# A two-layer graph convolution on one core: edge steps written out, gathers far ahead of the scatters, table clears interleaved with loads

## What is computed

```python
x = _layernorm(x + layer0(x, ...), axis=-1)
x = _layernorm(x + layer1(x, ...), axis=-1)
# in a layer:
h_s = s @ lin1_ws ;  h_v = einsum('nci,cd->ndi', v, lin1_wv)
w = silu(edge_scalars @ fc_w1) @ fc_w2
es = h_s[edge_src] ; ev = h_v[edge_src]        # gather by source
m_s1 = w1 * es * e0 ; m_v1 = (w2 * es)[:, :, None] * e1[:, None, :]   # and so on
agg = segment_sum(mid, edge_dst, num_segments=n)                      # scatter by destination
out = self connection of x + agg @ lin2, gated (layer 0) or scaled by alpha (layer 1)
```

## Time and profile before

| what | value |
|---|---|
| median of 3 runs | 2085.45 us (2083.66 to 2088.11) |
| span of the profiled execution | 2039.2 us |
| median less span, work that the span does not hold | 46.25 us |
| edge stage of layer 0, up to the first table read | 0 to 757 us |
| node stage of layer 0 | 757 to 1079 us |
| edge stage of layer 1 | 1079 to 1786 us |
| node stage of layer 1 | 1786 to 2039 us |

### The profile page before, as it was taken

One profiled execution on the slowest core, in us unless ns is written; L12 is line 12 of the kernel. 1 busy time (PEld: TensorE's weight loads), 2 busy tenths in 40 slices (PEclk: granted clock), 3 DMA queues, 4 the chain that ended last, 5 costly groups with the idle time before them and its releaser, 6 DMA issues.

```text
span 2039.2 us, 47736 instructions
## 1 busy us (share of the span) xinstructions
PE 1409.6 (69%) x10326; PEld 1244.3 (61%) x10326; DVE 1438.3 (71%) x5755; ACT 1048.9 (51%) x3502; POOL 1476.8 (72%) x1923
## 2 busy tenths in 40 slices
PE   5078887888888748888875999999998999300000
PEld 4067776777777637767654888888888888200000
DVE  5067777777777719999993666666666666299998
ACT  3034444444444418999983545445455445147766
POOL 4067888878888747888873677777777777468887
PEclk8589999998999969999987999999999999755555
DMA  9966666666666749999964777777777777499997
GB/s 388 429 155 134 135 138 135 136 133 136 137 134 135 178 102 333 338 340 337 337 221 131 167 170 170 169 168 174 170 172 169 169 173 163 84 366 401 403 399 290
DMA packets 253833, 439.51 MB, mean 216 GB/s; under 512 B 33424, under 2 KB 131152, under 8 KB 250576
## 3 DMA queue, kind: packets, MB, share of 16 engines
q1 hardware_dynamic: 152304, 311.47, 45.0%
q0 software_dynamic: 75264, 67.79, 24.0%
q10 hardware_dynamic: 26208, 59.65, 7.5%
HBM read 235.50 MB, written 203.27 MB: 215 GB/s over the span
## 4 chain that ended last, share of the span: by engine, by line
issue 23%; PE 19%; POOL 16%; DVE 11%; ACT 11%; another core or an unknown queue 6%; DMA 5%; SPq 5%; ACTq 2%; DVEq 1%; POOLq 0%
POOL table L500 7%; ACT y L849 6%; POOL xg L483 5%; DVE stats L1083 3%; SPq L374 3%; DVE res L1044 3%; DMA table<-sums,row_all 3%; PE ps L660 2%; PE ps L681 2%; POOL half_rstd L534 2%; DMA dst_row<-in_dst_row 2%; PE ps L641 2%; PE ps L627 1%; PE ps L643 1%
## 5 line engine op out<-in xcount | busy, mean ns | idle before, releaser
L500 POOL DMA_INDIRECT table<-sums,row_all x392 | 628.7, 1604 | 299.6 <-issue 131.0
L784 ACT COPY msg<-ps 128x192 f32<-128x192 f32 (+1 forms) x196 | 57.6, 294 | 703.5 <-PE ps L660 514.1
L849 ACT ACTIVATE y<-res,norm 128x160 f32<-128x160 f32 x756 | 330.2, 508 | 126.7 <-POOL norm L536 66.8
L993 DVE SCALAR_TENSOR_TENSOR x1g<-ps,a_all,x1g 128x160 f32<-128x160 f32 x392 | 132.4, 379 | 207.9 <-remote 139.7
L483 POOL DMA_INDIRECT xg<-in_x_rows,src_all x196 | 203.2, 1037 | 59.6 <-issue 58.1
L483 POOL DMA_INDIRECT xg<-x_rows,src_all x196 | 196.6, 1003 | 64.3 <-issue 57.3
L641 PE MATMUL ps<-weights,midT 128*128 128x128 f32 (+1 forms) x784 | 159.3, 286 | 67.6 <-DVE msg L953 67.0
L1083 DVE BATCH_NORM_STATS2 stats<-res 128x6 f32<-128x160 f32 x784 | 196.1, 312 | 2.6
L948 DVE TENSOR_TENSOR pe<-ps,ea_all 128x192 f32<-128x192 f32 x196 | 69.6, 355 | 166.8 <-ACT msg L784 89.7
L534 POOL TENSOR_TENSOR half_rstd<-var,minus_half 128x8 f32<-128x8 f32 x98 | 165.6, 1690 | 14.2
L641 PEld LDWEIGHTS ps<-weights,midT 128*128 128x128 f32 x784 | 123.8, 199 | 71.9 <-issue 64.4
(11 more groups left out here) (114 smaller groups left out, 4402.2 us busy)
## 6 DMA issues: line engine op xcount, KB each, us to landing
tab<-table SPq DMA_DIRECT2D x98, 384.0 KB, 5.2
table<-zeros SPq DMA_DIRECT2D x24, 1536.0 KB
table<-zeros SPq DMA_DIRECT2D x98, 324.0 KB
tab<-table SPq DMA_DIRECT2D x98, 324.0 KB, 5.6
xzT<-in_xzT SPq DMA_DIRECT2D x98, 320.0 KB, 4.9
x1g<-x_rows SPq DMA_DIRECT2D x98, 320.0 KB
base_rows<-x1g SPq DMA_DIRECT2D x98, 320.0 KB
x1g<-base_rows SPq DMA_DIRECT2D x98, 320.0 KB, 5.0
```

Source lines behind the costliest of these rows:

```text
L500: pool.indirect_dma_start(out=table[l], out_offset=bass.IndirectOffsetOnAxis(ap=row_all[:, at:at + 1], axis=0), in_=sums[j % 4][:, t, 0:W] ...
L849: last = nc.scalar.activation(y[u][:, t, :], res[u][:, t, :], ACT.Identity, scale=rstd[u][:, t:t + 1], bias=shift[u][:, t:t + 1])
L993: last = stt(x1g[v][:, 2 * b + t, :], n1_ps[:, t, :], a, x1g[v][:, 2 * b + t, :], ALU.mult, ALU.add)
```

## The change

`run_pairs` takes the place of `run_stages` in both edge stages on SP, PE, ACT and DVE: all 98 pairs are written out and there is no loop. The buffers of gathered rows grow from 8 to 30: 15 lie in the memory of `res` and 7 in that of `x1g`, tiles that the edge stages don't use otherwise (layer 1 uses the first four of `x1g`). The buffers of sums grow from 4 to 16, in the memory of `tab`. GpSimd gathers pairs up to `lead(l, n)` ahead of scatter n. SP loads `attrT` four pairs ahead, and clears table 0 with two transfers for each pair, each of which waits until the fourth transfer before it has landed.

```diff
+def run_pairs(base, stages):
+    for k in range(base, base + NP + max(lag for lag, _ in stages)):
+        for lag, f in stages:
+            if base <= k - lag < base + NP:
+                f(k - lag, k - lag - base, (k - lag) % RING)
...
+RES_SLOTS, X1_SLOTS = 15, 7
+XG_RING = RING + RES_SLOTS + X1_SLOTS
+SUM_RING = 16
+CLEARS0 = 25
...
+def lead(l, n):
+    return min(NP, 38 + n * 60 // 90 if l == 0 else 16 + n * 9 // 10)
...
+def clears0_by(m):
+    return 4 if m < 4 else min(CLEARS0, 4 + 2 * (m - 3))
...
+def clears1_by(m):
+    return max(0, min(NG, (m - 13) * NG // 82))
...
-                        for k in range(25):
+                        for k in range(clears0_by(m - 1) if m > 3 else 0, clears0_by(m)):
+                            if k >= 4:
+                                sp.wait_ge(s_zero0[k % 4], 16 * (k // 4))
...
-                    wait_count(pool, s_xgT, j - RING + 1)
+                    wait_count(pool, s_xgT, j - XG_RING + 1)
                     if l == 0:
-                        wait_count(pool, s_ea, j - RING + 1)
+                        wait_count(pool, s_ea, j - XG_RING + 1)
+                    if j >= RING:
+                        pool.wait_ge(s_gather[j % RING], landed(j - RING, j % RING, RING, 32))
...
-                for k in range(l * NP, (l + 1) * NP + RING):
-                    if k < (l + 1) * NP:
-                        gather(k)
-                    if k - RING >= l * NP:
-                        scatter(k - RING)
+                for n in range(NP):
+                    for k in range(lead(l, n - 1) if n else 0, lead(l, n)):
+                        gather(l * NP + k)
+                    scatter(l * NP + n)
```

More of the change, by code:

```diff
@@ L161, in program, with slots @@
         src_all = sb("src_all", [P, NP * 2], I32)
-        xg = [sb(f"xg{u}", [P, 2, D + 1]) for u in range(RING)]
+        res_all = sb("res_all", [P, RING * T * D])
+        x1g_all = sb("x1g_all", [P, RING * T * D])
+        tab_all = sb("tab_all", [P, RING * T * 192])
+        def slots(ap, n):
+            w = 2 * (D + 1)
+            return [ap[:, k * w:(k + 1) * w].rearrange("p (t c) -> p t c", t=2) for k in range(n)]
+        xg = ([sb(f"xg{u}", [P, 2, D + 1])[:, :, :] for u in range(RING)] + slots(res_all[:, :], RES_SLOTS) +
+              slots(x1g_all[:, 4 * T * D:RING * T * D], X1_SLOTS))
         attrT = eight("attrT", [P, P])
@@ L174, in program @@
         same1 = four("same1", [P, PAIR])
-        sums = four("sums", [P, 2, 192])
+        sums = [tab_all[:, k * 384:(k + 1) * 384].rearrange("p (t c) -> p t c", t=2) for k in range(SUM_RING)]
         prod = two("prod", [P, 2, 3 * V])
@@ L243, in program @@
         s_step = sem("constants_step")
-        s_zero = [sem(f"table{l}_zeroed") for l in range(2)]
+        s_zero0 = [sem(f"table0_zeroed{k}") for k in range(4)]
+        s_zero1 = sem("table1_zeroed")
         s_src = sem("src_loaded")
@@ L350, in _, with load_attr, load_attrs @@
                 base = l * NP
-                def load_attr(j, m, u, early=False):
-                    if l == 0 and isinstance(m, int) and 4 <= m < RING and not early:
-                        return
+                def load_attr(j, m):
                     wait_count(sp, s_hid, j - 7)
                     R2 = 2 * LAYERS[l]["R"]
-                    sp.dma_start(attrT[u][0:R2, :], A[f"attrT{l}"][bass.ds(m, 1)].rearrange("a k e -> k (a e)")).then_inc(s_attr[u], 16)
+                    sp.dma_start(attrT[j % RING][0:R2, :], A[f"attrT{l}"][m:m + 1].rearrange("a k e -> k (a e)")).then_inc(
+                        s_attr[j % RING], 16)
+                def load_attrs(j, m, u):
+                    if m == 0:
+                        for k in range(4):
+                            load_attr(j + k, k)
+                    if m + 4 < NP:
+                        load_attr(j + 4, m + 4)
                 def load_dst_row(j, m, u):
@@ L483, in gather @@
                         pool.indirect_dma_start(
-                            out=xg[j % RING][:, t, 0:width], out_offset=None, in_=rows,
+                            out=xg[j % XG_RING][:, t, 0:width], out_offset=None, in_=rows,
                             in_offset=bass.IndirectOffsetOnAxis(ap=src_all[:, at:at + 1], axis=0)).then_inc(s_gather[j % RING], 16)
@@ L494, in scatter @@
                     if j == l * NP:
-                        pool.wait_ge(s_zero[l], 16 * (25 if l == 0 else NG + 1))
+                        if l == 0:
+                            for k in range(4):
+                                pool.wait_ge(s_zero0[k], 16 * len(range(k, CLEARS0, 4)))
+                        else:
+                            pool.wait_ge(s_zero1, 16 * (NG + 1))
                     W = LAYERS[l]["ROW"]
@@ L770, in copy_z @@
                     wait_count(act, s_xgT, j - 1)
[L771 removed]
+                    copy(xz[u][:, :, :], xg[j % XG_RING][:, :, M:D]).then_inc(s_xz, 1)
                 def copy_xT(j, m, u):
```

62 lines of the change are left out of this document (31 added, 31 removed).

## The result

The changed kernel takes 2167.98 us (median of 4 runs, 2161.89 to 2177.17); the kernel before took 2085.87 us beside it. The ratio is 1.0397, with a 95% interval of 1.0365 to 1.0429: 4% slower, where no change was forecast, and outside the range.

A forecast was written before the change was run, and what follows sets the result against it. Two chains were taken to hold a pair: POOL's issue, some 6.45 us, and scatter after scatter, some 6.2. The terms +17 - 13.6 + 1 - 5 = -0.6 us gave 2084.9 us, own range 2074 to 2097, wider range 2062 to 2104.

The forecast's parts named there:

- from first to last scatter of layer 0: Layer 0's 97 steps: 60 with gathers at 6.57 us, 37 without at 6.25; -13.6 us, bounds -16 to -2.
- The sentence on the tail: Layer 0, behind the last gather: steps without gathers priced at 6.25 us, as clears of table 1 ran there too.
- First scatter: Start of layer 0: gathers and loads slow the clears, first scatter at about 125.7 us; +17 us, bounds +5 to +27.
- Layer 1: Layer 1's 97 steps: 642 us instead of 647.1, -5 us, bounds -12 to +2.
- eight between at 6.4: Layer 1: eight steps between the 82 with gathers and the last seven without, priced at 6.4 us each, 51.2 us.
- The fill: Layer 1, first gather to first scatter: four attrT loads now stand ahead of the first x1 load; +1 us.
- 46.25 us "around the span": Whole kernel: difference of the 2039.2 us span and the 2085.45 median, taken as unchanged.
- (a): Rival, edge stages: fetching the written-out code becomes the bound; slower, about 2122 us; chance 10%.
- (b): Rival, start: clears and gathers add up, +27, 2095 us; 2104 with steps without gathers at 6.5; chance 15%.
- (c): Rival: steps with gathers fall to 6.43 us, 2059; or clears lose nothing to gathers, 2073; chance 15% for both.
- (d): Rival, layer 0: the gathers' issue counts in full, saving 77 us, near 2010 us; chance 4%.
- (e): Rival: the lead does nothing, clears end as before and steps stay as they are; 2085 us; chance 5%.

The follow-up runs named there:

- unroll_no_pace: unroll_only without SyncE's wait, in layer 0, for scatter m-8 to land before it issues table 1's clear; 2173.63 us, ratio 1.0467.
- lead9_paced: clears_run_lead9 with one wait per pair for a scatter, ahead of layer 0's clears and in layer 1 ahead of the loads; 2041.48 us, ratio 0.982.
- unroll_only: The kernel before with the edge steps of both layers written out and nothing else; 2069.63 us, ratio 0.9996.
- clears_run_lead9: clears_run with gathers 9 pairs ahead in both layers, keeping 30 buffers of rows and 16 of sums; 2159.01 us, ratio 1.0422.
- clears_run: The changed kernel with table 0's clears in one run at pair 3, as before the change; 2177.37 us, ratio 1.0509.
- before_again: The kernel before, unchanged, timed and profiled anew; 2071.54 us, ratio 0.9994, its profiled execution 2072.37 us.

## Why the prediction was wrong

**The step that failed is the second, "from first to last scatter of layer 0", -13.6 us.** It took 53.2 us more instead. The prediction took the landing of a scatter to be as late as before, 6.20 to 6.57 us in every step. In the changed kernel 34 of the 77 steps counted had a clear beside the scatter and took 7.98 us, 1.49 more than the others; that is 51 of the 53 us. What was missed is that the diff dropped the wait in `clear_table1`. The prediction counted on table 1's clears to be harmless, since "clears of table 1 ran in it too"; those clears had been kept clear of the scatters by the wait. unroll_no_pace takes out that wait alone and layer 0's steps go from 638.2 to 734.4 us; lead9_paced puts it back and they go from 725.4 to 644.0.

The sentence on the tail was also a misreading. Its rows are those from 729 us on the earlier trace rows, and the last nine clears of table 1 had all been issued by then, in one run from 701.48 to 708.87:

```profile
701.48 7.39 SPq L381 DMA_DIRECT2D table<-zeros  x9
```

Nor is the idle of 5.19 us at 710.74 due to the end of the loop: with the loops written out the step at that place was still 8.27 us (unroll_only; 8.65 before). That those nine clears cause it was not tested.

The price of a step without gathers was nearly right where nothing disturbs it. In the changed kernel the undisturbed steps without gathers took 6.35 us if one of 9.02 is left out (ten steps), against the 6.25 of the sum; those with gathers took 6.46 (32 steps), and the last three of the layer 6.1 to 6.2. So the gathers do lie almost wholly inside the wait for the landing.

**First scatter: the mechanism was right, the size off.** +17 was forecast, +22.9 came, within the bounds of 5 and 27, with 11 pairs summed by then, as forecast; clears_run_lead9, with 9 pairs of gathers, has it at 109.6. The gathers' part was right: in clears_run, where no load stands among the clears, the `dst_row` just behind them comes at 121.58 instead of 108.71, +12.9, and the sum had 5.0 MB / 0.425 = 11.8. What was sized too low is the loads of pairs 4 to 14 among the clears: 5.2 us in the sum, some 10 by an estimate, the difference of 131.62 and 121.58. In the stretch 50:54 the hardware queue moved 1.36 MB in 4 us beside gathers and loads, where the sum took 1.45:

```profile
q1 hardware_dynamic: 298, 1.36, 83.9%
q0 software_dynamic: 148, 0.27, 18.2%
```

**Layer 1: -5 was forecast for its steps, +65.3 measured against the profile of before**, but only +20.1 against before_again (712.4 and 692.3). The 6.64 us a pair on which the sum stood is a pace that this kernel seldom has. Some 10 of the 20 us lie in one step, from scatter 91 to scatter 92, which took 16.74 us:

```profile
1863.45 0.99 POOL L536 DMA_INDIRECT res_all<-x_rows,src_all  x1 [0.30 <-issue]
1875.13 1.62 POOL L557 DMA_INDIRECT table<-tab_all,row_all  x1 [10.69 <-ACT tab_all L856]
```

With `lead(1, n)` = 16 + 9 n / 10 the lead shrinks to 6 pairs, and the last gather goes only behind scatter 91; on TensorE the sum of pair 92 stands behind the turn of that last pair, and ACT waited 8.6 us for its rows. The step took 16.1 to 17.2 us in all six runs with this lead, and no step of layer 1 took over 9.8 in those with a constant lead of 9 pairs. The prediction's "eight between at 6.4" took no account of it. In clears_run_lead9, which differs from clears_run in the lead alone, layer 1's steps are 24 us shorter. The fill, from layer 1's first gather to its first scatter, was forecast at +1 and came to -8.0, or +1.5 against before_again (38.9). In the changed kernel it is not the first sum that ends it but POOL's own 32 gathers: the scatter at 1194.68 follows them with 0.30 us of idle.

**The 46.25 us "around the span" do not exist.** In every profiled execution with a time beside it they are 1.7 to 1.8 us. The prediction had a span of 2039.2 beside a median of 2085.45 and took the difference as fixed overhead; it was the sign that the profiled execution was of another kind than the timed ones, and it hid that layer 1 had slow steps which could be won. Some 13 us of it, from the 2072.37 of before_again's profiled execution to 2085.45, stay unexplained.

**The rivals.** (a), fetching code, is refuted by unroll_only. (b) had the right sign and half of the first term, but not the place of the loss: its "steps without gathers at 6.5" was 6.99 (6.35 undisturbed), and the steps with gathers, which it left at 6.57, took 7.23. (c) and (d) did not come; POOL's idle of 2.75 us behind undisturbed scatters at 823.96 is what stood against (d). "The lead does nothing" (e) did not come either: clears_run and clears_run_lead9, which differ in the lead alone, show the greater lead 24 us later at the first scatter and 24 us longer in layer 1's steps.

## What to carry to other kernels

When a chain of DMAs that wait for each other's landing sets the pace, look where the other transfers fall in its step. Here the clears and loads cost nothing 5 to 6 us behind the first scatter DMA, little within 0.5 us of it, and 2 us at 2 to 3 us behind it. A wait that guards no data may be what holds them in place: before removing one, look in the timeline at what is issued behind it and when. Where the profiled span and the timed median differ by more than the 2 us seen here, find out first which of the two executions is being read. Gathering far ahead costs what the gathers take from the transfers that the first step waits for, and brings little if they lay inside another wait; and the lead must not run out before the last pair, or the pipeline empties there.

## What the runs showed that was not expected

One program has two paces in layer 1: its steps with gathers took 6.68 us in one profile and 7.21 in the other, with the same instructions, by where its loads had settled in the step. A single wait for each pair in SP's queue gave the quick pace in the profile and in all five timed executions (2028 to 2039 us), and the lowest time here, 2032.05 us against 2071.49.

Writing out all edge steps raised the instruction packets from 57 to 172 and moved the time by nothing (0.9996, 0.9976 to 1.0015).

A second scatter DMA with a clear of 324 KB and two loads issued within 1 us behind it made the next scatter come 9.62 us behind the first (399.34 to 408.96) instead of 6.5, 3.1 us late and so more than the 2 us in which those transfers were moved. What adds to it, and why a store of 320 KB at the same place (`base_rows`) costs 0.2 us at most, was not tested.
